# Selective-scan kernel: VectorE alone empties the bank of delta, one wide absolute value, relu moved into the last wide operation, the front begun at step 4, and a narrower wait for a turned buffer

## The reference

```
xc    = silu(conv4(x_in) + conv_b)
delta, Bm, Cm = split(xc @ x_proj_w.T)            # ranks 64, 16, 16
dt    = softplus(delta @ dt_w.T + dt_b)
h_t   = exp(dt_t * A) * h_{t-1} + (dt_t * xc_t) * B_t     # 16 states a channel
y_t   = sum over states (h_t * C_t) + D * xc_t
```

## Time and profile before

| | us |
|---|---|
| median of 3 runs | 4224.65 |
| lowest and highest | 4217.56 and 4225.96 |
| span of the profiled execution | 4222.2 |
| of it the scan's recurrences (line 718), from the first to the last start | 257.9 to 1944.9 |

### The profile page before, as it was taken

One profiled execution on the slowest core, in us unless ns is written; L12 is line 12 of the kernel. 1 busy time (PEld: TensorE's weight loads), 2 busy tenths in 40 slices (PEclk: granted clock), 3 DMA queues, 4 the chain that ended last, 5 costly groups with the idle time before them and its releaser, 6 DMA issues. The chain is left out here.

```text
span 4222.2 us, 69815 instructions
## 1 busy us (share of the span) xinstructions
PE 3401.3 (81%) x22940; PEld 2121.0 (50%) x22940; DVE 2787.7 (66%) x4369; ACT 2464.7 (58%) x3860; POOL 1886.3 (45%) x1761
## 2 busy tenths in 40 slices
PE   8567878878788787885876999999999976599980
PEld 4146666666666666664553333333333335366660
DVE  3258888888888888886764777777777727100105
ACT  3268888888888888884220555665566552122110
POOL 1048888888888888885541000010001015200006
PEclk9679999999999999998995999999999996799995
DMA  6533333333333333334634001011001025122205
GB/s 204 156 101 91 91 91 91 91 91 91 92 91 89 93 91 89 91 93 183 236 119 120 9 19 19 7 19 22 17 9 19 9 64 189 34 83 83 83 31 188
DMA packets 158040, 357.64 MB, mean 85 GB/s; under 512 B 20931, under 2 KB 65974, under 8 KB 143216
## 3 DMA queue, kind: packets, MB, share of 16 engines
q1 hardware_dynamic: 125392, 266.42, 22.8%
q0 software_dynamic: 16784, 52.10, 3.5%
q10 hardware_dynamic: 15504, 34.61, 2.2%
HBM read 253.24 MB, written 102.26 MB: 84 GB/s over the span
## 5 line engine op out<-in xcount | busy, mean ns | idle before, releaser
L506 POOL TENSOR_TENSOR scan_hC<-scan_hh,scan_cbc 128x512 f32<-128x512 f32 x1024 | 1382.8, 1379 | 160.1 <-DVE scan_hh L718 101.4
L718 DVE TENSOR_TENSOR_SCAN scan_hh<-scan_dA,scan_state,scan_bx 128x512 f32<-128x512 f32 x1024 | 1252.4, 1264 | 213.9 <-PE scan_bx L810 99.5
L810 PE MATMUL scan_bx<-kept_ident,scan_dBxT 128*128 128x128 f32 x4096 | 677.3, 292 | 197.5 <-DVE scan_hh L718 133.5
L1561 PE MATMUL attend_s<-attend_kt,attend_qt 32*128 32x512 f32 (+3 forms) x2560 | 793.7, 609 | 33.9 <-DMA attend_qt<-attend_zero 27.6
L559 ACT ACTIVATE scan_dBxT<-scan_dtxT,scan_bt 128x512 f32<-128x512 f32 x1028 | 655.7, 711 | 81.6 <-PE scan_bx L810 81.4
L820 PE MATMUL scan_acc<-kept_ident,scan_hC 128*128 128x128 f32 x4128 | 656.8, 287 | 56.1 <-ACT scan_uu L568 29.3
L810 PEld LDWEIGHTS scan_bx<-kept_ident,scan_dBxT 128*128 128x128 f32 x4096 | 502.4, 150 | 389.7 <-DVE scan_hh L718 232.1
L554 ACT ACTIVATE scan_dA<-scan_dt,scan_an 128x512 f32<-128x512 f32 x1028 | 660.9, 712 | 29.1 <-DVE scan_hh L718 29.1
L1582 PE MATMUL attend_s<-attend_qt,attend_kt 32*128 32x512 f32 (+3 forms) x2560 | 635.7, 581 | 17.9 <-POOL attend_pb L1438 14.6
L1472 DVE TENSOR_REDUCE attend_mx<-attend_s 128x1 f32<-128x512 f32 x768 | 494.5, 686 | 197.0 <-PE attend_s L1561 195.8
L1532 ACT ACTIVATE attend_pb<-attend_s 128x1024 f32<-128x1024 f32 x384 | 390.8, 1024 | 279.1 <-PE attend_s L1582 279.1
(11 more groups left out here) (207 smaller groups left out, 3675.1 us busy)
## 6 DMA issues: line engine op xcount, KB each, us to landing
scan_xs<-scratch_xin SPq DMA_DIRECT2D x288, 256.0 KB, 6.2
scan_cbc<-scratch_crows SPq DMA_DIRECT2D x64, 1024.0 KB, 4.8
scratch_y<-scan_uu ACTq DMA_DIRECT2D x17, 1024.0 KB
scratch_xin<-proj_out_x SPq DMA_DIRECT2D x8, 1024.0 KB
scratch_sz<-proj_out_z SPq DMA_DIRECT2D x8, 1024.0 KB
scratch_exp_in<-proj_cleared SPq DMA_DIRECT2D x8, 1024.0 KB, 8.4
mix_yf<-scratch_y SPq DMA_DIRECT2D x8, 1024.0 KB, 6.6
mix_yb<-scratch_y SPq DMA_DIRECT2D x8, 1024.0 KB, 9.5
```

The lines of the kernel that those rows point to most:

```text
L506: pool.tensor_tensor(hC[n % 2][:, m, :], h[:, m, :], rows, ALU.mult).then_inc(hc_ok, 1)
L718: dve.tensor_tensor_scan(hh[n % 2][:, m, r], dA[n % 2][:, m, r], bx[bank(j)][:, r], state[:, d, n, m:m + 1], ALU.mult, ALU.add).then_inc(h ...
L810: last = pe.transpose(bx[bank(j)][:, t * P:(t + 1) * P], dBxT[turned_slot(n)][:, t, m * P:(m + 1) * P], k["ident"][:, :])
L1561: pe.matmul(s1[v % S1][:, 0:w], qt[n % SETS][rows, t * P:(t + 1) * P], kt_[n % SETS][rows, c * C:c * C + w], start=True, stop=True).then_i ...
```

## The change

VectorE alone reads the bank of delta: it adds the bias and writes the sum to `dt`, with no maximum, and frees the bank. ScalarE takes the absolute value afterwards, as one instruction on 128x2048 from `dt` to `ee`. GpSimd's wide addition now adds e and the logarithm instead of e and relu (into `ee`), after the logarithm and after step 7. The maximum with 0 is in VectorE's `softplus`. The places in the order move: `proj` to slots 4 to 7, `turn_bc` to 11, `dt_of` to 14, 16, 18, 20, `evacuate` to step 1, `proj_out` to 2, `bt_out` to 3, the absolute value to the tail of step 5, exp to 6, 1+e to its tail, the logarithm to 7. VectorE's three wide operations come after steps 9, 10 and 11. TensorE's adds: two a slot in slots 0 to 3, none in 4 to 8, two in slot 9, then one a slot. ScalarE's wait at n = 15 asks for `f*64 + 64 + turned_free(0)`, which is 52 injects of the unit.

```diff
--- before.py
+++ after.py
@@ -373,7 +373,7 @@
         bx = [s.ps(f"bx{i}", [P, C]) for i in range(3)]
         fr = s.ps("fr", [P, C])
         loaded_x = s.sems("loaded_x0", "loaded_x1")
-        (picked, relu_ok) = s.sems("picked", "relu_ok")
+        (picked, abs_ok) = s.sems("picked", "abs_ok")
...
         LAG = 8
-        AT_DT, AT_NEXT, AT_TURN, AT_SKIP = (18, 21, 24, 27), (29, 33, 38, 43), (49, 51, 53, 55), (14, 16, 19, 22)
+        AT_PROJ, AT_BT, AT_DT = 4, 11, (14, 16, 18, 20)
+        AT_NEXT, AT_TURN, AT_SKIP = (29, 33, 38, 43), (49, 51, 53, 55), (13, 17, 19, 22)
...
-            def front_relu_and_e(d, g):
-                pool.wait_ge(e_ok, g + 1)
-                pool.tensor_tensor(dt[d][:, :, :], dt[d][:, :, :], ee[:, :, :], ALU.add).then_inc(v_ok, 1)
-
-            front_relu_and_e(0, 0)
+            def front_log_and_e(g):
+                pool.wait_ge(ln_ok, g + 1)
+                pool.tensor_tensor(ee[:, :, :], ee[:, :, :], dtx[:, :, :], ALU.add).then_inc(v_ok, 1)
+
+            front_log_and_e(0)
             with pool.Fori(0, B) as b:
...
-                            if n == 6:
-                                front_relu_and_e(1 - d, f + 1)
+                            if n == 7:
+                                front_log_and_e(f + 1)
...
-            def dt_out(d, f, m, group):
-                if m == 0 and not (isinstance(f, int) and f == 0):
+            def front_abs(d, f, group):
+                if not (isinstance(f, int) and f == 0):
 
                     act.wait_ge(dt_ok, f)
-                act.wait_ge(relu_ok, f * DT + m + 1)
-                act.activation(ee[:, m, :], fr[:, :], ACT.Abs, bias=db[:, d, m:m + 1]).then_inc(fr_out, 1)
-
-            def front_exp(f, group):
-
                 act.wait_ge(fr_out, group + 1)
+                act.activation(ee[:, :, :], dt[d][:, :, :], ACT.Abs).then_inc(abs_ok, 1)
+
+            def front_exp(f):
+
+                act.wait_ge(abs_ok, f + 1)
                 act.activation(ee[:, :, :], ee[:, :, :], ACT.Exp, scale=-1.0).then_inc(e_ok, 1)
 
...
-            for m in range(DT):
-                dt_out(0, 0, m, 6 + m)
-            front_exp(0, 9)
+            front_abs(0, 0, 9)
+            front_exp(0)
...
                 def middle(n):
-                    if n == 2:
+                    if n == 1:
                         for half in range(2):
                             evacuate(f, half)
+                    if n == 2:
+                        proj_out(g, first + FR_PROJ)
                     if n == 3:
-                        proj_out(g, first + FR_PROJ)
-                    if n == 4:
                         bt_out(o, first + FR_BT)
-                    if n in (5, 6):
-                        dt_out(o, g, n - 4, first + FR_DT + n - 4)
+                    if n == 6:
+                        front_exp(g)
                     if n == 7:
-                        front_exp(g, first + FR_DT + 3)
-                    if n == 8:
+                        front_log(g)
+
+                def tail(n):
+                    if n == 2:
+                        store(f)
+                    if n == 5:
+                        front_abs(o, g, first + FR_DT + 3)
+                    if n == 6:
                         front_one_plus(g)
-                    if n == 9:
-                        front_log(g)
-
-                def tail(n):
-                    if n == 3:
-                        store(f)
-                    if n == 4:
-                        dt_out(o, g, 0, first + FR_DT)
-                    if n == 6:
-                        dt_out(o, g, 3, first + FR_DT + 3)
                     if n == 12:
                         silu(d, f + 2, first + FR_NEXT + 3)
 
@@ -624,7 +620,10 @@
                     dn, at = (d, n + 1) if n + 1 < NS else (o, 0)
                     if n + 1 == NS:
                         act.wait_ge(fr_out, first + FR_TURN + JT)
-                    act.wait_ge(bx_mm, f * SUB + turned_free(n + 1 if n + 1 < NS else NS))
+                    if n + 1 < NS:
+                        act.wait_ge(bx_mm, f * SUB + turned_free(n + 1))
+                    else:
+                        act.wait_ge(bx_mm, f * SUB + SUB + turned_free(0))
                     spread_b(dn, at)
...
-            def softplus_low(d, f):
+            def softplus_low(f):
 
                 dve.wait_ge(u_ok, f + 1)
                 dve.wait_ge(v_ok, f + 1)
-                dve.scalar_tensor_tensor(out=ee[:, :, :], in0=uu[:, :, :], scalar=-1.0, in1=dt[d][:, :, :],
+                dve.scalar_tensor_tensor(out=ee[:, :, :], in0=uu[:, :, :], scalar=-1.0, in1=ee[:, :, :],
                                          op0=ALU.add, op1=ALU.subtract).then_inc(d_ok, 1)
 
             def softplus(d, f):
-                dve.wait_ge(ln_ok, f + 1)
                 dve.wait_ge(d_ok, f + 1)
-                dve.scalar_tensor_tensor(out=dt[d][:, :, :], in0=dtx[:, :, :], scalar=0.0, in1=ee[:, :, :],
+                dve.scalar_tensor_tensor(out=dt[d][:, :, :], in0=dt[d][:, :, :], scalar=0.0, in1=ee[:, :, :],
                                          op0=ALU.max, op1=ALU.subtract).then_inc(dt_ok, 1)
...
-            def relu(d, f, m, group):
+            def dt_out(d, f, m, group):
                 if m == 0 and not (isinstance(f, int) and f == 0):
                     dve.wait_ge(dt_ok, f)
                 dve.wait_ge(fr_mm, group + 1)
-                dve.tensor_scalar(dt[d][:, m, :], fr[:, :], db[:, d, m:m + 1], 0.0, ALU.add, ALU.max
-                                  ).then_inc(relu_ok, 1)
+                dve.tensor_scalar(dt[d][:, m, :], fr[:, :], db[:, d, m:m + 1], None, ALU.add).then_inc(fr_out, 1)
...
-                    if n == 8:
-                        softplus_low(o, g)
                     if n == 9:
+                        softplus_low(g)
+                    if n == 10:
                         softplus(o, g)
-                    if n == 10:
+                    if n == 11:
                         times_x(o, g)
...
-            FIRST = 11
-            adds = {j: [j - LAG] for j in range(SUB) if not LAG <= j < 2 * FIRST - LAG}
-            for j in range(FIRST, 2 * FIRST - LAG):
-                adds[j] = [2 * (j - FIRST), 2 * (j - FIRST) + 1]
+            adds = {j: [2 * j - LAG, 2 * j - LAG + 1] for j in range(LAG // 2)}
+            adds[LAG + 1] = [0, 1]
+            for j in range(LAG + 2, SUB):
+                adds[j] = [j - LAG]
...
-                    if 7 <= j < 11:
-                        proj(o, g, first + FR_PROJ, [j - 7])
-                    if j == 15:
+                    if AT_PROJ <= j < AT_PROJ + DT:
+                        proj(o, g, first + FR_PROJ, [j - AT_PROJ])
+                    if j == AT_BT:
                         turn_bc(first + FR_BT)
```

More of the change, by code:

```diff
@@ L595, in middle @@
                 def middle(n):
[L596 removed]
+                    if n == 1:
                         for half in range(2):
                             evacuate(f, half)
+                    if n == 2:
+                        proj_out(g, first + FR_PROJ)
                     if n == 3:
[L600 to L601 removed]
                         bt_out(o, first + FR_BT)
[L603 to L604 removed]
+                    if n == 6:
+                        front_exp(g)
                     if n == 7:
[L606 to L609 removed]
                         front_log(g)
                 def tail(n):
[L613 removed]
+                    if n == 2:
                         store(f)
[L615 to L616 removed]
+                    if n == 5:
+                        front_abs(o, g, first + FR_DT + 3)
                     if n == 6:
[L618 removed]
+                        front_one_plus(g)
                     if n == 12:
@@ L699, in _ @@
             for m in range(DT):
-                relu(0, 0, m, 6 + m)
-            softplus_low(0, 0)
+                dt_out(0, 0, m, 6 + m)
+            softplus_low(0)
             softplus(0, 0)
@@ L730, in unit @@
                             i = AT_DT.index(at)
-                            relu(o, g, i, first + FR_DT + i)
+                            dt_out(o, g, i, first + FR_DT + i)
                         if at in AT_NEXT:
```

1 line of the change is left out of this document (removed).

## The result

The changed kernel takes **4194.84 us** (median of 4 runs, 4189.89 to 4208.22), against 4223.45 of the kernel before beside it. The ratio is 0.9937, with a 95% interval of 0.9919 to 0.9956: faster by 0.6%, not the 1.7% forecast. The direction was right and the number inside the stated range, but the gain is 29 us where 73 was expected, less than half.

What follows compares the result with a forecast made beforehand. Bound: hand-overs between three almost equally loaded engines. Unit 105.55 - 99.75 = 5.8, less 0.9, is 4.9 us; times 16 = 78.4, less 2.1 and 3, gives 73: 4151 us, 8-in-10 range 4090 to 4208.

Steps and rivals of the forecast that it cites:

- The layout of the first half: Slots 0 to 32 of the new unit: slot 14 starts at 19.7 us, slot 32 at 48.1, 1.7 late.
- The pairs of slots with a product of delta: Around delta's four products: TensorE needs some 3.6 us a pair against VectorE's 3.0, so 0.6 is lost three times.
- the terms for the tail: Slots 48 to unit end: slot 48 at 77.2, 0.4 us for slots 49 to 51, boundary wait gone, end at 99.75.
- its bounds for clock and absolute value: Clock loss of 0 to 4 us a unit and absolute value 0 to 0.9, giving a range of 4136 to 4205.
- the bound that was argued from slot 19: ScalarE's absolute value waits for the reading after slot 20, decays ahead for slot 19: at most about 2 us.
- the sum's third quarter: Slots 32 to 47, two readings and VectorE's three wide operations: 29.1 us, slot 48 at 77.2, another 1.3 gained.
- signs of being wrong: Clock near 0.5 in slots 0 to 20, line 666 waiting for GpSimd, long absolute-value wait, or unit above 103 us.
- its 0.9 us: Allowance a unit for TensorE's half clock after idling ahead of delta's first product, and for idle times too small to list.
- A: Only the boundary pays; ScalarE's regained lead is eaten at bt_out and by the logarithm: 28 us gained, 4197; chance 0.18.
- its 2.09 us: VectorE's wait at the unit's end for the inject of slot 0, claimed to go with the narrower turned-buffer wait.
- C: Slower: TensorE at half clock at unit start, slots 0 to 7; unit 107.9 us, about 4263 in all; chance 0.08.
- D: It does not act: GpSimd sets the pace, its wide addition blocks as before; within 0.2%, 4224; chance 0.06.

Runs made afterwards that it cites:

- run 3: The changed kernel without GpSimd's wide addition of e and the logarithm; softplus_low takes the smaller of e and minus the logarithm: 4175.38 us.
- run 1: The kernel before with only ScalarE's narrower wait for the turned buffer: 4155.8 us, ratio 0.9842.
- run 5: The changed kernel with the front (proj, turn_bc, delta's products, evacuation and what follows on ScalarE) back at its old, later step: 4160.81 us.
- Run 12: The changed kernel with turn_bc and the products of delta two slots later: 4192.58 us.
- runs 9 and 10: Four turned buffers instead of three, the first on the changed kernel (4175.16 us), the second on the kernel of run 5 (4129.34 us).

## Why the prediction was wrong

**The layout of the first half was nearly right.** Slot 14 was put at 19.7 and measured 20.1; slot 32 at 48.1 and measured 49.4. The wait at slots 4 to 7 of 1 us behind the paired adds and proj is there (1.0 at 883.45), and so is the one at slot 14, ended by TensorE's inject behind bt_out, and one at slot 32 that ends with a decay, 2.14 instead of 1.7. The pairs of slots with a product of delta take 3.8 to 3.9 us each and not 3.65; three of them make 0.7. Its working has slips, all small: the terms for the tail as written give 99.56 at the unit's end, not 99.75; the 29.1 of slots 32 to 47 is right with the three readings that stand there (after 33, 38 and 43), not two; and its bounds for clock and absolute value give 4215 at the top, not 4205. ScalarE's wait for the absolute value is 2.0, the bound that was argued from slot 19. The absolute value's own 1.92 us against 1.90 is right.

**The step that failed is the sum's third quarter, under GpSimd.** It took the three wide operations at 2.26, 2.95 and 3.10 as they stood in the rows of before. Part of such a duration is a wait for GpSimd's instruction in progress, which depends on where in a product the operation begins and on how much stands behind it. The 2.26 was the favourable case, with nothing waited for; in the new order it is 4.4. Softplus takes 0.4 more and times_x 0.5 less. Slots 32 to 47 were forecast at 29.1 and took 30.97, and run 3, where softplus_low meets no wait, took 29.26. The prediction named a cover of 7 us between the addition and softplus_low. It held, and the wait came in another form: not for the addition, but for the products behind it. That the backlog the late addition leaves is what makes VectorE wait longest is argued from the timeline and from run 3; no run moved the backlog alone. Both of the prediction's signs of being wrong that bear on this came: a wait of this operation for GpSimd, and a unit above 103 us.

**The tail was too cheap.** 0.4 us stood for slots 49 to 51; the quarter took 23.50 where 22.55 was forecast. The idle time ahead of slots 49 and 51 is 1.4 in the mean, against 0.3 in the kernel before. The half clock after times_x is most of the reason (0.50 granted from 958 to 963, with the estimate and the units of run 1 above). It was seen in advance as a mechanism, but its 0.9 us were put elsewhere in the unit: at slot 14, where the clock stayed full (1.00 from 885 to 895 with an idle time of 1.24 us in it, and the product at 895.88 takes 1.12 as in the earlier trace rows). The Trainium skill's rule that the prediction cites, half clock by default and full clock by activity, agrees with the trace after the 3.78 us; after the shorter idle times these rows show nothing lost.

These make 0.4 + 0.9 + 1.9 + 0.95, about 4.1 us a unit over the layout's 99.75, where 0.9 was allowed: 3.2 too little, or 51 us over 16 units, for 44 in the medians.

**The rivals.** A, "only the boundary pays", gives almost the measured number, 4197, and as an account of the changed kernel it is nearer than the forecast: it had the regained lead eaten at bt_out and by the logarithm, with VectorE waiting at slots 14 and 32 as long as before at 18 and 36, and the means are 1.95 and 2.14 against 1.78 and 1.39. Its number is still partly luck, for it has nothing of the waits of some 6 us a unit that did go (slots 12, 15, 21, 24, 27 and 29), nor of the new ones at slots 4, 16, 20, 49 and under GpSimd that took their place. And its name is wrong: run 1 shows that the boundary with the lead behind it is worth 67 us, twice what A gave it, and run 5 that the early front gives back 34. The prediction let each part be judged against the kernel before as it stood; it never priced the narrower wait with the order left alone, and its 2.09 us for it left out what the lead saves at slot 12. C did not come: the granted clock was 1.00 from slot 0 to slot 13 (877.54 to 895), and so in every other unit from 2 to 15 but one, with 0.97. D is refuted by run 1.

**Why the early front costs.** It asks for bt_out and delta's product four slots sooner, while ScalarE gets no further ahead: evacuation, proj_out and bt_out stand in its queue in the same order with the same decays and spreads between. Run 12 moves the wait and gains nothing to speak of; runs 9 and 10 give ScalarE more lead and gain 20 and 31 us. What it brings at the far end (exp and logarithm sooner) is eaten at slot 32. That the wide activations, which follow each other within two steps, have used up the lead there is argued from ScalarE's order. Whether another spacing of those three would help was not tried.

## What to carry to other kernels

When several edits come together, price the smallest one alone first: here one corrected wait was worth more than the whole change, and its gain hid the loss of the rest. The view of waits names the releaser that came last by the profile; check it against the slot before it is summed. In a pipeline of equally loaded engines a lead is what pays, and an order that asks for a result sooner than its engine can give it only moves the wait. A duration read from a trace can hold a wait: compare it with the same instruction where nothing runs beside it (2.29 us ahead of the loop, on line 665, against 4.4 in it) before it is used for another order.

## What the runs showed of the hardware

A wide VectorE operation on two SBUF operands and GpSimd's products or copies took their time one after the other in all 16 units, though their records overlap: the later one lasted its own time plus the rest of the other's, so a GpSimd copy of 0.2 us became 2.29. The operation did not always win at the first end of a GpSimd instruction: begun at 937.75, it was passed over when the product ended at 938.75 and got through at 939.9. So it went on line 665 of the changed kernel in 15 of 16 units. In the kernel before lines 672 and 677 got through at the first in all 16. What decides this stays open.
